# A decoder layer's second half: 32-row tiles for the context scores, an fp16 expert bias, per-head exponentials and the upper half of gelu on ScalarE

## What is computed

```python
x = layernorm(x + self_attention(x))                     # 16 heads of 32
q, k, v = heads(x @ Wq + bq), heads(ctx @ Wk + bk), heads(ctx @ Wv + bv)
scores = q @ k.T / sqrt(32)                              # 16 heads, 77 columns each
x = layernorm(x + softmax(scores + mask * -1e9) @ v @ Wo + bo)
logits = cosine(x, centroids) + x @ w_route.T            # 8 experts
gates = softmax(keep_top_2(logits))
h = gelu(x @ w1[e] + b1[e])                              # 256 wide per expert
out = sum over e of gates[e] * (h @ w2[e] + b2[e])
x = layernorm(x + out)
```

## Time and profile before

| what | us |
|---|---|
| median of 3 runs | 2633.9 (2633.06 to 2635.76) |
| profiled execution | 2630.97 |
| its span, first to last instruction | 2629.2 |
| TensorE busy | 2430.0 (92%) |
| VectorE busy | 1715.9 (65%) |
| GpSimd busy | 1119.8 (43%) |
| ScalarE busy | 1097.3 (42%) |

### The profile page before, as it was taken

One profiled execution on the slowest core, in us unless ns is written; L12 is line 12 of the kernel. 1 busy time (PEld: TensorE's weight loads), 2 busy tenths in 40 slices (PEclk: granted clock), 3 DMA queues, 4 the chain that ended last, 5 costly groups with the idle time before them and its releaser, 6 DMA issues. The chain is left out here.

```text
span 2629.2 us, 42902 instructions
## 1 busy us (share of the span) xinstructions
PE 2430.0 (92%) x13556; PEld 1018.3 (39%) x13556; DVE 1715.9 (65%) x3957; ACT 1097.3 (42%) x2066; POOL 1119.8 (43%) x404
## 2 busy tenths in 40 slices
PE   8999799999999999999956799999999999999998
PEld 3444223332333233323213354444445454454543
DVE  4443687776777677767405477767677776767665
ACT  4331256665666566666623242332324232322420
POOL 0000379988898989898952111102111111101100
PEclk9999799999999999999977899999999999999999
DMA  7864312212121212140021101010100101010000
GB/s 250 294 212 156 89 38 54 58 42 59 42 58 42 63 38 76 28 111 20 25 93 60 45 1 62 1 46 18 41 22 1 63 1 46 17 45 17 1 17 17
DMA packets 130506, 155.66 MB, mean 59 GB/s; under 512 B 19838, under 2 KB 98174, under 8 KB 129245
## 3 DMA queue, kind: packets, MB, share of 16 engines
q1 hardware_dynamic: 130269, 152.69, 18.9%
HBM read 99.96 MB, written 52.17 MB: 58 GB/s over the span
## 5 line engine op out<-in xcount | busy, mean ns | idle before, releaser
L762 ACT ACTIVATE probs<-st_ps 128x512 f32<-128x512 f32 (+3 forms) x1280 | 605.3, 536 | 359.0 <-PE st_ps L865 206.6
L637 POOL TENSOR_TENSOR total<-total,probs 128x2048 f32<-128x2048 f32 (+3 forms) x200 | 706.3, 3531 | 77.8 <-ACT probs L762 65.6
L804 DVE TENSOR_REDUCE seg_max<-s_ps 128x1 f32<-128x512 f32 x768 | 506.2, 684 | 143.4 <-PE s_ps L851 139.9
L865 PE MATMUL st_ps<-q_pair,k_pair 98*128 98x512 f16 (+3 forms) x1280 | 445.5, 362 | 36.6 <-ACT probs L762 22.7
L851 PE MATMUL s_ps<-k_pair,q_pair 96*128 96x512 f16 (+3 forms) x1280 | 446.0, 363 | 31.9 <-DMA q_pair<-q_parts 11.2
L1429 PE MATMUL fps<-x2T,w_p_hi 128*128 128x512 f16 x1024 | 317.3, 379 | 0.0
L885 PE MATMUL o_ps<-probs,v_sb 128*32 128x512 f32 (+3 forms) x2560 | 309.0, 556 | 0.0
L808 DVE CUSTOM_DVE_ANT_0 s_ps<-s_ps,later 128x384 f32<-128x384 f32 (+3 forms) x512 | 250.4, 497 | 89.1 <-issue 85.9
L1429 PE MATMUL fps<-w_p_hi,hT 128*128 128x512 f16 x1024 | 306.1, 381 | 0.0
L865 PEld LDWEIGHTS st_ps<-q_pair,k_pair 98*128 98x128 f16 x1280 | 124.8, 99 | 357.7 <-ACT probs L762 264.7
L1133 POOL TENSOR_TENSOR rstd<-rstd,keep_power 128x4 f32<-128x4 f32 x24 | 26.1, 1090 | 552.0 <-DVE rstd L1254 552.0
(11 more groups left out here) (164 smaller groups left out, 3403.8 us busy)
## 6 DMA issues: line engine op xcount, KB each, us to landing
k_pair<-k_parts SPq DMA_DIRECT2D x96, 128.0 KB, 3.6
q_pair<-q_parts SPq DMA_DIRECT2D x96, 128.0 KB, 4.7
x_raw<-xT_in SPq DMA_DIRECT2D x8, 1024.0 KB, 6.3
q_parts<-qk_out SPq DMA_DIRECT2D x32, 256.0 KB, 3.6
k_parts<-qk_out SPq DMA_DIRECT2D x32, 256.0 KB, 3.9
piece_raw<-w_in SPq DMA_DIRECT2D x8, 1024.0 KB, 8.7
v_rows<-v_out SPq DMA_DIRECT2D x32, 256.0 KB, 2.2
w_parts<-piece_cut SPq DMA_DIRECT2D x8, 1024.0 KB, 5.6
```

Of the source, the lines that this page charges most:

```text
L637: last = nc.gpsimd.tensor_tensor(summed[:, :, off:], other[:, :, off:], probs[:, k % NP, :, off:], ALU.add)
L762: nc.scalar.activation(probs[:, k % NP, h, off:], st_ps[:, p % (2 * NVU) % RING, off:], ACT.Exp, scale=SCALE).then_inc(exp_done.sem, 1)
L804: nc.vector.reduce_max(highest, s_ps[:, slot], AX.X).then_inc(s_read.sem, 1)
L865: last = nc.tensor.matmul(st_ps[:, slot, off:], k_pair[a][:, h, kt * P:(kt + 1) * P], q_pair[a][:, c, h, off:], start=True, stop=not diagonal)
```

## The change

- The context's keys are stored as they are (128 x 77 per head group) and not as a block-diagonal matrix. A scores stage does 16 matmuls of 32 rows and 77 columns, head h of each group in rows 32h to 32h+31, its result in bank h; VectorE's mask addition reads one bank per h and writes every fourth head.
- VectorE negates the maximum (a 128 x 16 operation) and subtracts nothing. ScalarE exponentiates each head by itself with the negated maximum as bias and the sum as accumulated output; VectorE's sum is gone.
- ScalarE writes the upper half of gelu behind each gelu; VectorE keeps the remainder.
- The expert bias is done in fp16: gates and b2 are split in halves and laid out in 96 rows, so that one f16 matmul gives all terms. VectorE makes the halves of the gates ahead of the gate stage's transpose, which is now a matmul with an fp16 identity. b2's halves are made in `project`.
- `PLAN` moves two units: turn1 3 to 4, scores1 7 to 6, scores2 7 to 6, route 4 to 5.

```diff
-                    act.wait_ge(cleared, 1)
                     act.wait_ge(ctx_loaded, 48)
                     for g in range(NG):
                         n = NUMBER["key", u, g]
                         act.wait_ge(prod_ready, n + 1)
-                        for h in range(HG):
-                            rows = slice(h * DH, (h + 1) * DH)
-                            last = nc.scalar.activation(
-                                blocks[rows, :, g, h * S2:(h + 1) * S2],
-                                prod[rows, n % NB, 0:KVC].rearrange("p (b s) -> p b s", b=B), ACT.Identity,
-                                bias=bk_sb[rows, g:g + 1])
-                        last.then_inc(act_took, 1)
+                        nc.scalar.activation(key_rows[:, :, g], prod[:, n % NB, 0:KVC].rearrange("p (b s) -> p b s", b=B),
+                                             ACT.Identity, bias=bk_sb[:, g:g + 1]).then_inc(act_took, 1)
...
+                if u == 3:
+                    dve.wait_ge(b2_loaded, 48)
+                    nc.vector.tensor_scalar(S["b2_parts"][:], b2_raw[:], XS, None, ALU.mult).then_inc(b2_ready, 1)
+                    dve.wait_ge(b2_ready, 1)
+                    nc.vector.scalar_tensor_tensor(b2_lo[:], b2_raw[:], XS, S["b2_parts"][:], ALU.mult,
+                                                   ALU.subtract).then_inc(b2_ready, 1)
+                    dve.wait_ge(b2_ready, 2)
+                    nc.vector.tensor_copy(S["b2_parts"][DH:2 * DH], b2_lo[DH:2 * DH]).then_inc(b2_ready, 1)
+                    dve.wait_ge(consts, 4)
+                    nc.vector.tensor_copy(S["ident16"][:], S["ident"][:]).then_inc(b2_ready, 1)
...
-    PLAN = [("out", 1), ("norm1", 2), ("turn1", 3), ("query", 1), ("scores0", 3), ("scores1", 7), ("scores2", 7),
+    PLAN = [("out", 1), ("norm1", 2), ("turn1", 4), ("query", 1), ("scores0", 3), ("scores1", 6), ("scores2", 6),
             ("scores3", 6), ("probs0", 0), ("probs1", 1), ("pv0", 1), ("probs2", 0), ("pv1", 1), ("probs3", 0),
-            ("pv2", 3), ("pv3", 1), ("out2", 6), ("norm2", 3), ("turn2", 2), ("route", 4), ("gate", 0)]
+            ("pv2", 3), ("pv3", 1), ("out2", 6), ("norm2", 3), ("turn2", 2), ("route", 5), ("gate", 0)]
...
-                    act.wait_ge(shifted.sem, at(shifted, i, u, j))
-                    nc.scalar.activation(soft[:, j], soft[:, j], ACT.Exp).then_inc(exped.sem, 1)
+                    act.wait_ge(negated.sem, at(negated, i, u, j))
+                    for h in range(H):
+                        last = nc.scalar.activation(soft[:, j, h], soft[:, j, h], ACT.Exp, bias=smax[:, j, h:h + 1],
+                                                    accum_out=ssum[:, j, h:h + 1])
+                    last.then_inc(exped.sem, 1)
...
+                    act.wait_ge(gelu_done.sem, at(gelu_done, i, u, n))
+                    if j == 0:
+
+                        act.wait_ge(f_ready.sem, at(f_ready, i, u, UNITS.index(("expert", e - 2, TT - 1)) if e >= 2
+                                                    else UNITS.index(("expert", E + e - 2, TT - 1)) - NUNIT))
+                    nc.scalar.activation(hT[:, 0, e % 2, j], hidden[:, n % 2], ACT.Copy, scale=XS).then_inc(h_hi.sem, 1)
...
-                for g in range(NG):
-                    bank = wait_product(i, u, AT_S + j * NG + g)
+                for h in range(HG):
+                    bank = wait_product(i, u, AT_S + j * HG + h)
                     nc.vector.scalar_tensor_tensor(
-                        soft[:, j, g * HG:(g + 1) * HG], bank[:, 0:KS].rearrange("p (h s) -> p h s", h=HG), SCALE,
-                        mask_sb[:].rearrange("p (a s) -> p a s", a=1).broadcast_to([P, HG, S2]), ALU.mult,
+                        soft[:, j].rearrange("p (g h) s -> p g h s", h=HG)[:, :, h],
+                        bank[:, 0:NG * S2].rearrange("p (g s) -> p g s", g=NG), SCALE,
+                        mask_sb[:].rearrange("p (a s) -> p a s", a=1).broadcast_to([P, NG, S2]), ALU.mult,
                         ALU.add).then_inc(dve_read.sem, 1)
-                dve.wait_ge(dve_read.sem, at(dve_read, i, u, nth(USES, AT_S + j * NG + NG - 1)))
+                dve.wait_ge(dve_read.sem, at(dve_read, i, u, nth(USES, AT_S + j * HG + HG - 1)))
                 nc.vector.reduce_max(smax[:, j], soft[:, j], AX.X).then_inc(smaxed.sem, 1)
                 dve.wait_ge(smaxed.sem, at(smaxed, i, u, j))
-                nc.vector.tensor_tensor(soft[:, j], soft[:, j], smax[:, j].rearrange("p (h a) -> p h a", a=1)
-                                        .broadcast_to([P, H, S2]), ALU.subtract).then_inc(shifted.sem, 1)
+                nc.vector.tensor_scalar(smax[:, j], smax[:, j], -1.0, None, ALU.mult).then_inc(negated.sem, 1)
 
             def softmax_end(i, u, j):
                 dve.wait_ge(exped.sem, at(exped, i, u, j))
-                nc.vector.reduce_sum(ssum[:, j], soft[:, j], AX.X).then_inc(ssummed.sem, 1)
-                dve.wait_ge(ssummed.sem, at(ssummed, i, u, j))
                 nc.vector.reciprocal(ssum[:, j], ssum[:, j]).then_inc(inverted.sem, 1)
...
-                    nc.vector.tensor_tensor(gates[:], weight[:], wide, ALU.mult).then_inc(routed.sem, 1)
+                    nc.vector.scalar_tensor_tensor(gates[:], weight[:], GS, wide, ALU.mult,
+                                                   ALU.mult).then_inc(routed.sem, 1)
                     nc.vector.scalar_tensor_tensor(gates_un[p][:], weight[:], UN, wide, ALU.mult,
                                                    ALU.mult).then_inc(gated.sem, 1)
+                    dve.wait_ge(routed.sem, at(routed, i, u, 12))
+                    nc.vector.tensor_copy(gate_parts[:, :, 0, 0:E], gates[:])
+                    nc.vector.tensor_copy(gate_parts[:, :, 1, 0:E], gates[:]).then_inc(routed.sem, 1)
+                    dve.wait_ge(routed.sem, at(routed, i, u, 13))
+                    nc.vector.tensor_tensor(gate_parts[:, :, 2, 0:E], gates[:], gate_parts[:, :, 0, 0:E],
+                                            ALU.subtract).then_inc(routed.sem, 1)
...
-                    dve.wait_ge(gelu_done.sem, at(gelu_done, i, u, n))
-                    if j == 0:
-
-                        dve.wait_ge(f_ready.sem, at(f_ready, i, u, UNITS.index(("expert", e - 2, TT - 1)) if e >= 2
-                                                    else UNITS.index(("expert", E + e - 2, TT - 1)) - NUNIT))
-                    nc.vector.tensor_scalar(hT[:, 0, e % 2, j], hidden[:, n % 2], XS, None,
-                                            ALU.mult).then_inc(h_hi.sem, 1)
...
-                    nc.vector.tensor_tensor(x2[q][:, j], bank, x2[q][:, j], ALU.add).then_inc(added.sem, 1)
+                    nc.vector.scalar_tensor_tensor(x2[q][:, j], bank, 1.0 / (GS * XS), x2[q][:, j], ALU.mult,
+                                                   ALU.add).then_inc(added.sem, 1)
...
+                    banks = [chain_bank(i, u, AT_S + j * HG + h) for h in range(HG)]
                     for g in range(NG):
-                        bank = chain_bank(i, u, AT_S + j * NG + g)
-                        nc.tensor.matmul(bank[:, 0:KS], xq[:, g, j * P:(j + 1) * P], keys[:, g], start=True,
-                                         stop=True).then_inc(c_ready.sem, 1)
+                        for h, bank in enumerate(banks):
+                            rows = slice(h * DH, (h + 1) * DH)
+                            last = nc.tensor.matmul(bank[:, g * S2:(g + 1) * S2], xq[rows, g, j * P:(j + 1) * P],
+                                                    keys[rows, g], start=True, stop=True)
+                            if g == NG - 1:
+                                last.then_inc(c_ready.sem, 1)
...
-                        last = nc.tensor.transpose(bank[0:E, j * P:(j + 1) * P], gates[:, j], ident[:])
+                        last = nc.tensor.matmul(bank[0:3 * DH, j * P:(j + 1) * P],
+                                                gate_parts[:, j].rearrange("p a e -> p (a e)"), W["ident16"][:],
+                                                start=True, stop=True)
...
-                    last = nc.tensor.matmul(bank, gT[u][:, j], W["b2_sb"][:], start=True, stop=True)
+                    last = nc.tensor.matmul(bank, gT[u][:, j], W["b2_parts"][:], start=True, stop=True)
```

More of the change, by code:

```diff
@@ L141, in project @@
         piece_hi, piece_lo = sem("piece_hi"), sem("piece_lo")
-        consts, cleared, squared, norm_ready, cent_ready, route_ready = (sem(n) for n in (
-            "consts", "cleared", "squared", "norm_ready", "cent_ready", "route_ready"))
+        b2_loaded, b2_ready = sem("b2_loaded"), sem("b2_ready")
+        consts, squared, norm_ready, cent_ready, route_ready = (sem(n) for n in (
+            "consts", "squared", "norm_ready", "cent_ready", "route_ready"))
         block = stack.enter_context(nc.Block())
@@ L207, in _ @@
                 if u == 2:
+                    sp.wait_ge(consts, 1)
+                    for r in range(3):
```

(13 more changed lines are left out.)

56 lines of the change are left out of this document (29 added, 27 removed).

## The result

The changed kernel takes 2660.6 us (median of 4, 2660.3 to 2663.2), the kernel before 2633.5 on the same chip: ratio 1.0103, 95% interval 1.0088 to 1.0119. Forecast were 2682 and slower. The loss is +27 us where +48 was forecast.

A forecast was written before the change was run, and what follows sets the result against it. TensorE, busy 92% of the span, was taken as the bound. Full slots +56, query -19, last slot's bias -3, first slot +5 + 0.6, clock +8 gave +48 on 2631.0: 2679, median 2682 us; 8 in 10: 2640 to 2755.

The forecast's parts named there:

- The loop: Score stages: last expert unit waits for a gelu queued behind exponentials; 16.5 us a turn against 11.3 of TensorE's work.
- X: ScalarE's time for 16 per-head exponentials per 128 tokens: 6.4 us, bounds 4.0 and 9.1.
- The price of a head: ScalarE's spacing of one per-head exponential with memory bias and accumulator read: 0.40 us, between 0.34 and 0.46.
- The prediction's own alternative for X = 5.4: Score stages with cheaper exponentials: TensorE waits 11.6 us a slot, against 15.2 in the forecast.
- the walk: Following score stages 0 to 3 through ScalarE, VectorE and TensorE: TensorE waits of 4.5 + 5.2 + 5.5 = 15.2 us a slot.
- the shorter bias: Expert bias, four units a chunk, as one f16 pass on TensorE: -3.1 us in each of eight slots.
- Scores on TensorE: Score matmuls as 32 row-tiled instructions side by side: about 0.9 us a stage instead of 2.07, saving 4.7 a slot.
- the series rival: Score matmuls' row tiles not running side by side: 3.4 us a stage, 25 us more, 2707 us; chance 0.11.
- Query wait: TensorE's 3.69 us wait ahead of the query projection in four slots should go: -19 us; rival that it stays 0.12.
- Gate: TensorE's 1.77 us wait at the gate grows by 0.6 us for VectorE's added work, eight times: +5 us.
- First slot: First chain, without experts: scores to turning of the probabilities 33.5 us instead of 28.6, +5 us.
- Clock: TensorE's clock halves behind the new score-stage waits, uncovered only behind stage 3: +1.2 x 7 = +8 us.

The follow-up runs named there:

- e2: Changed kernel with the 16 per-head exponentials kept but without accumulated sums, VectorE summing again: 2640.6 us.
- e5: Changed kernel with the unit plan of before (turn1 3, scores1 7, scores2 7, route 4): 2665.1 us.
- e4: Changed kernel with ScalarE issuing the exponentials of score stages 0 to 2 behind the stage's gelus instead of ahead, no work removed: 2597.5 us.
- e6: Changed kernel with the expert bias put back to one f32 matmul of 8 rows, and the gates' transpose with it: 2679.2 us.
- e9: Changed kernel with the score matmuls issued head by head (same 32 rows in a row) instead of group by group: 2686.0 us.
- e3: Changed kernel with VectorE writing the upper half of gelu again instead of ScalarE: 2670.3 us.
- e10: e4 with VectorE writing the upper half of gelu again instead of ScalarE: 2600.6 us.

## Why the prediction was right, point by point

*The loop: right.* Forecast 16.5 us for X = 6.4, and by the same sum (X + 1.3 + 8.85) 15.65 for X = 5.5; measured 15.53 at X = 5.5. e2 (14.04) and e5 (16.18) move it by the amounts of one ScalarE and one VectorE term, and e4 takes it apart by order alone.

*The price of a head: mis-sized.* 0.40 us was taken between 0.34 and 0.46, it is 0.343. The lower row was the right one, the spacing of the Square pairs with the memory bias added; the run of 16 short ones at 0.396 (32 partitions, from PSUM) misled. The prediction's own alternative for X = 5.4, waits of 11.6 us a slot, gives (-4.7 - 3.1 + 0.6 + 11.6) x 7 = +31, with -19 - 3 + 1.6 + 8 for the rest +18: 2652. The point was 21 us too high: this term makes 30 of it, and some 9 come back from others. The next part gives 6.7 of them; the score stages, 51.6 us in mean where the walk gives 50.6, give 7 more, so smaller terms must stand against them, which no run separates.

*The wait ahead of the first scores: missed.* The bias unit that shrank had covered ScalarE's eviction of xq: 0.96 us in each of seven slots, +6.7. I had costed the shorter bias at its full 3.1 us without asking what it hid; e6 shows the cover coming back.

*Scores on TensorE: right in kind.* 1.13 us instead of 0.9 against 2.07; the series rival (25 us more) is out. e9 measures the edit that it describes at 25.4, and that the two agree is luck: the rival took 3.4 us a stage and counted two stages, the run has 2.65, and from that I expected 12 to 20.

*Query wait: gone in the changed kernel,* as forecast, and back in e3. The second remainder, which I put 0.3 us ahead of GpSimd, started 0.28 to 0.41 us ahead of it in the seven full slots and took 0.69. e3 puts the whole part at 9.7 us; with the 7 us that its score stages gave back, the wait and what follows it are worth about 17, near the 19. e10 shows that this depends on what stands around it.

*Gate: right.* 1.77 to 2.29 us. The fifth unit ahead of it covers nothing: e5, with four, waits as long.

*First slot:* from the first scores to the turning 29.2 us (28.6 before), +0.6 instead of +5, nearly all of it as X is smaller (the same sum gives 29.9 for X = 5.5).

*Clock: right in kind, its size not separated.* It halves in the score stages, as here in the changed kernel behind a wait of 2.26 us; columns as in the earlier trace rows:

```profile
1999.50:2003.00 3.50, 3.50 (x26) 1.65 (x28) 2.37 (x4) 3.05 (x4) 0.00 (x0) 0.51 0.00 0
2003.00:2006.00 3.00, 3.00 (x32) 1.56 (x29) 2.96 (x7) 0.00 (x0) 0.00 (x0) 1.00 0.02 5
```

But behind an equal wait in the slot before (1847.68) the next scores ran at full speed. The mean granted clock bounds the size: it is 0.958 before, 0.949 in the changed kernel and 0.958 in e4, and what is missing to 1, times the span, is 110, 136 and 109 us. So the change cost up to 25 us of full clock, part of it in waits or covered by VectorE, where it costs nothing, and e4 gave it back. The gain of e4 fits: TensorE's waits for `fps` banks fall by 42 us (31.3 + 25.6 to 14.7) of the 63, and most of the rest is open to the clock. No run isolates it; the 8 us remain an estimate, and may be low.

## What to carry to other kernels

When work is moved to an engine that is idle most of the time, its place in that engine's order counts before its length: 5.5 us ahead of a gelu cost 63 us more than the same 5.5 us behind it. Before costing a shortened instruction at its full saving, look for the wait that it covered on another engine. A loop through two or three engines is worth walking, since with the measured exponentials it gave the turn to about 0.1 us; then check every term for which leg it lies on, as a unit moved into a waiting engine's slack (e5) can lengthen another leg.

## What the runs showed of the hardware

An accumulator read behind a short exponential adds 0.09 us to the spacing (0.25 in e2, 0.343 in the changed kernel), though it lasts 0.19. 32 score instructions (f32 loads of 128 columns, 77 columns streamed) take 1.13 us when the four row groups alternate and 2.65 us when the same rows follow one another, both at full clock. Behind waits of 2.0 to 2.3 us TensorE's clock was at half for 3.4 to 6.8 us in some slots of the changed kernel, e4 and e5 and at full speed in others. VectorE's rounding to f16 of 128x512 took 4.7 us instead of 0.42 where it started 0.11 to 0.19 us after GpSimd's addition of 128x2048, which took 4.6.
